# A two-layer recurrent, attention and expert network on one core: the rotation of queries and keys made a lane of its own with one PSUM bank

## The reference, cut to what matters

```python
xn = _layernorm(x)
s = _L0_attn_ref(xn, ...)      # gated recurrence: x@W1, gates, scan over the 512 tokens, @W2
g = _silu(_L0_ffn_ref(xn, ...))  # two layers, below
x = x + s * g
xn = _layernorm(x)
s = _L1_attn_ref(xn, ...)      # 16 heads, all 512 tokens against all 512 tokens
g = _silu(_L1_ffn_ref(...))    # an expert MLP, whose result here is used for one sample
x = x + s * g

def _layer(x, wqkv, qs, ksc, wo, lg, lb, w1, b1, w2, b2):    # run twice
    h = shift_token(x)
    q, k, v = split(h @ wqkv, 3)                 # 8 heads of 64
    q = l2norm(q) * qs;  k = l2norm(k) * ksc
    q, k = rotary_xpos(q, k)                     # rotation by tables of cos and sin
    o = local_attention(q, k, v)                 # windows of 64 tokens and the one before
    x = x + o @ wo
    h = layernorm(shift_token(x)) * lg + lb
    a, g = split(h @ w1 + b1, 2)
    return x + (a * gelu(g)) @ w2 + b2
```

## Time and profile before

| | |
|---|---|
| median of three runs | 3840.28 us |
| the profiled execution: its own time | 3830.7 us |
| the profiled execution: its span | 3828.9 us |
| PE busy | 3102.7 us, 81% |
| DVE busy | 2714.3 us, 71% |
| ACT busy | 2401.6 us, 63% |
| POOL busy | 933.2 us, 24% |
| TensorE clock granted, mean | 0.929 of full |

### The profile page before, as it was taken

The page is one execution under the profiler, slowest core; times in us unless marked ns, Lnnn a source line. Parts: engine busy times, 40 slices in busy tenths (PEclk is TensorE's granted clock), DMA queues, the critical chain, the costliest instruction groups (busy, mean ns, idle before and its releaser), DMA issues.

```text
span 3828.9 us, 55334 instructions
## 1 busy us (share of the span) xinstructions
PE 3102.7 (81%) x19984; PEld 1603.7 (42%) x20144; DVE 2714.3 (71%) x4829; ACT 2401.6 (63%) x5082; POOL 933.2 (24%) x685
## 2 busy tenths in 40 slices
PE   4668787888978787887978888897878789797786
PEld 2444443434444443444444344444444344444241
DVE  3476777868687886868687786868778686868432
ACT  2345666766666675766667676666667676666553
POOL 2021322222122322222132222213232221223100
PEclk7779898999999999999999899999989999999997
DMA  2001000010101001010100101010100101010200
GB/s 68 1 4 46 16 30 32 20 53 16 53 16 50 16 22 47 20 49 20 49 20 26 36 20 53 16 53 16 42 20 20 53 19 50 18 49 13 92 26 11
DMA packets 113451, 122.82 MB, mean 32 GB/s; under 512 B 13427, under 2 KB 86685, under 8 KB 113181
## 3 DMA queue, kind: packets, MB, share of 16 engines
q1 hardware_dynamic: 113180, 119.26, 9.7%
HBM read 64.70 MB, written 54.53 MB: 31 GB/s over the span
## 4 chain that ended last, share of the span: by engine, by line
PE 52%; DVE 26%; ACT 11%; issue 6%; POOL 5%; SPq 1%; DMA 0%; DVEq 0%; POOLq 0%; ACTq 0%
PE pb L573 29%; PE o_bank L573 12%; POOL scratch L1390 4%; DVE nmax L1292 4%; PE s L573 4%; PE pb L668 3%; PE pb L699 2%; DVE stat L1216 2%; ACT ex L1022 2%; DVE scratch L1220 2%; DVE scratch L1196 2%; DVE stat L1186 2%; PE pb L723 2%; DVE side L1158 1%; DVE scratch L1230 1%
## 5 line engine op out<-in xcount | busy, mean ns | idle before, releaser
L1022 ACT ACTIVATE ex<-s,nmax 128x512 f32<-128x512 f32 x1024 | 698.3, 686 | 279.7 <-DVE nmax L1292 257.1
L1292 DVE TENSOR_REDUCE nmax<-s 128x1 f32<-128x512 f32 x1024 | 676.2, 680 | 259.8 <-PE s L573 257.1
L573 PE MATMUL o_bank<-ex,vsc 128*64 128x512 f32 x2048 | 528.2, 638 | 84.6 <-POOL vsc L1424 84.2
L1424 POOL TENSOR_TENSOR vsc<-vrow,rinv 128x256 f32<-128x256 f32 x256 | 157.0, 613 | 1724.2 <-DVE rinv L1300 1724.2
L1385 POOL TENSOR_TENSOR scratch<-scratch 128x1024 f32<-128x1024 f32 x128 | 307.1, 2399 | 564.5 <-DVE scratch L1199 538.5
L573 PE MATMUL s<-qs,ks 96*128 96x512 bf16 x1024 | 345.2, 394 | 82.7 <-ACT ex L1022 82.7
L573 PE MATMUL pb<-wqkv,hsh 128*128 128x512 f32 x768 | 379.1, 622 | 33.8 <-DVE hsh L1179 26.1
L573 PE MATMUL pb<-kT,qT 64*64 64x64 f32 (+1 forms) x6144 | 330.8, 257 | 45.1 <-DVE scratch L1220 12.7
L959 ACT ACTIVATE scratch<-scratch 128x512 f32<-128x512 f32 x256 | 160.7, 628 | 321.1 <-DVE scratch L1220 321.0
L668 PE MATMUL pb<-const,scratch 128*128 128x128 f32 x1024 | 165.3, 308 | 242.2 <-POOL scratch L1390 242.2
L573 PEld LDWEIGHTS pb<-kT,qT 64*64 64x64 f32 x6144 | 282.9, 144 | 98.4 <-issue 98.4
(11 more groups left out here) (190 smaller groups left out, 6108.9 us busy)
## 6 DMA issues: line engine op xcount, KB each, us to landing
parts_store<-side SPq DMA_DIRECT2D x64, 384.0 KB, 2.6
qs<-parts_store SPq DMA_DIRECT2D x128, 192.0 KB, 2.7
ks<-parts_store SPq DMA_DIRECT2D x128, 192.0 KB, 3.2
parts_store<-side SPq DMA_DIRECT2D x64, 256.0 KB, 2.9
parts_store<-side SPq DMA_DIRECT2D x64, 128.0 KB, 2.7
xin<-in_L_attn_x SPq DMA_DIRECT2D x16, 256.0 KB, 3.6
out<-o1T SPq DMA_DIRECT2D x16, 256.0 KB, 4.3
wqkv<-in_L_ffn_wqkv SPq DMA_DIRECT2D x1, 1536.0 KB
```

The lines of the kernel that those rows point to most:

```text
L573: return pe.matmul(o, l, r, start=start, stop=stop, skip_group_check=True)
L1022: A(ex[:, w % 2, j, :], s_bank[(2 * NT + c) % SIMS][:], ACT.Exp, bias=nmax[:, c % 8:c % 8 + 1], accum_out=rsum[:, w % 2, j:j + 1]).then_in ...
L1292: V.tensor_reduce(nmax[:, c % 8:c % 8 + 1], s_bank[(2 * NT + c) % SIMS][:], X, ALU.max, negate=True).then_inc(GV, 1)
L1424: G.tensor_tensor(vsc[:, w % 2].rearrange("p (m a) d -> p m a d", a=2), vrow[:, m:m + 2, 2 * V1 * p:2 * V1 * (p + 1)].rearrange("p m (a d) ...
```

## The change

- The steps from `shift` to `tk` leave `attn0`/`attn1` and become flows `qkv0`/`qkv1`. What stays in `attn` is the score units, `oturn` and `wo`, with unchanged banks A, B, C.
- `q`, `k`, `v`, `tq` and `tk` all use one new bank E. Each waits until the one before has been copied out of it. To make room for E the sims have two banks instead of three.
- Lanes: p is `qkv1`(i-1), `qkv0`(i). r is `attn1`(i-1), `attn0`(i), `post0`(i). s is `pre`(i), `gru`(i-1), `post1`(i-1), `keep0`. g is `glob`(i-2) heads 2 to 15 with its end, `keep1`, then `glob`(i-1) `values` and heads 0 and 1 (FIRST = 2). `expert` moves from iteration 16 to 17, which also holds heads 2 to 15 of the last sample. So an iteration starts with layer 1 of one sample and ends with layer 0 of the next.
- ACT copies q and k out of PSUM at once, and squares both from the copy in one instruction of 128 by 1024. The square is written where the cosine product will be (`l_sq = l_c`), so for t > 0 it waits for the POOL addition of the tile before. `l_qk` has one buffer instead of two, so the copy of q of a tile waits for the sine products of the tile before.
- The score units get scratch of their own (scratch grows from 6144 to 7168 columns); `qT`, `kT`, `va` are still single, so layer 0 of a sample waits piece by piece for the score units of layer 1 of the sample before. `xn0` gets two buffers.
- SP issues the loads of heads 6 to 15 ahead of the stores of the new parts, and the weights of the experts after them.

```diff
-SIMS = 3
+FIRST = 2
-def attn_steps():
+def qkv_steps():
     s = [("shift",)]
...
-    s += [("score", 0), ("rot2", NT - 1), ("tq", NT - 1), ("tk", NT - 1)]
-    units = 2 * NT
+    return s + [("rot2", NT - 1), ("tq", NT - 1), ("tk", NT - 1)]
+
+
+def attn_steps():
+    s, units = [], 2 * NT
     for u in range(units + 4):
-        if 0 < u < units:
-            s += [("score", u)]
         if u < units:
-            s += [("prob", u)]
+            s += [("score", u), ("prob", u)]
...
-    half = s.index(("sim", H1 // 2, 0))
+    half = s.index(("sim", FIRST, 0))
...
-        "a": lane("attn0", 0, STEPS["attn0"]) + lane("post0", 0, STEPS["post0"]) + lane("attn1", 0, STEPS["attn1"]),
-        "s": lane("post1", -1, STEPS["post1"]) + lane("keep0", 0, [("x0",)]) + lane("gru", 0, STEPS["gru"])
-        + lane("pre", 1, STEPS["pre"]),
-        "x": lane("expert", -B, STEPS["expert"][:-1]),
+        "p": lane("qkv1", -1, STEPS["qkv1"]) + lane("qkv0", 0, STEPS["qkv0"]),
+        "r": lane("attn1", -1, STEPS["attn1"]) + lane("attn0", 0, STEPS["attn0"]) + lane("post0", 0, STEPS["post0"]),
+        "s": lane("pre", 0, STEPS["pre"]) + lane("gru", -1, STEPS["gru"]) + lane("post1", -1, STEPS["post1"])
+        + lane("keep0", 0, [("x0",)]),
+        "x": lane("expert", -B - 1, STEPS["expert"][:-1]),
         "g": lane("glob", -2, second) + lane("keep1", -1, [("x1",)]) + lane("glob", -1, values + first),
...
 ORDER = {
-    "pe": ("ga5g2asag2a4gsg5aga2gas3ag3s2a3gsas3gs3a3g3a2g5a2gagsg2ags3g2a2g3agsa2g2as3asg4ag3asa2ga2ga4xg3x4ga2"
...
+    "pe": ("3xgp6xg11xs2gpgs5x2gp2xgsgpgxspgpsgspg4xp2gxrprpxgxprsgxspg7xps2grp3rp2gxp2gxg2xr4xprpgrgx2gxrxrp2xr"
...
+            def qkv_does(l, b, s):                                   # PE
+                f, kind, t = qkv[l], s[0], s[1]
+                if kind in ("q", "k", "v"):
+                    if kind == "v":
+                        need(pe, f, "act", b, ("k", t), "c")
+                    elif kind == "k":
+                        need(pe, f, "act", b, ("q", t), "c")
+                    elif t >= 2:
+                        need(pe, f, "act", b, ("tk", t - 2), "t")
...
+                    mm(bank_e, hsh[:, P * t:P * t + P], wqkv[:, l, INNER * n:INNER * (n + 1)]).then_inc(f.sem["pe"], 1)
...
                 if kind in ("q", "k"):                               # ACT
                     t, k = s[1], int(kind == "k")
-                    src = bank_b if k else bank_a
+                    if t and kind == "q":
+                        need(act, f, "dve", b, ("rot", t - 1), "s1")
                     need(act, f, "pe", b, s, "p")
-                    if t:
-                        need(act, f, "dve", b, ("rot", t - 1), "ss")
-                    A(l_sq[:, INNER * k:INNER * (k + 1)], src, ACT.Square).then_inc(FA, 1)
-                    if t >= 2:
-                        need(act, f, "dve", b, ("rot", t - 2), "s1")
-                    A(l_qk[t % 2][:, INNER * k:INNER * (k + 1)], src, ACT.Copy).then_inc(FA, 1)
+                    A(l_qk[:, INNER * k:INNER * (k + 1)], bank_e, ACT.Copy).then_inc(FA, 1)
+                    if k:
+                        if t:
+                            need(act, f, "pool", b, ("rot", t - 1), "add")
+                        need(act, f, "act", b, s, "c")
+                        A(l_sq, l_qk, ACT.Square).then_inc(FA, 1)
...
-                    if c >= SIMS:
-                        need(pe, glob, "act", b, ("sim", (c - SIMS) // 4, (c - SIMS) % 4), "e")
+                    if c >= 2:
+                        need(pe, glob, "act", b, ("sim", (c - 2) // 4, (c - 2) % 4), "e")
```

246 lines of the change are left out of this document (123 added, 123 removed).

## The result

The changed kernel took 3775.77 us (median of four runs, 3771.37 to 3777.48), the kernel before beside it 3839.36 us: ratio 0.9834, 95% interval 0.9816 to 0.9851. It is faster by 1.7%, where 4.2% were forecast. The profiled execution has a span of 3769.6 us.

The account below looks back on a forecast made before the run. The kernel was taken as bound by the chain attn0, post0, attn1. Parts of 116, 74 and 22 us sum to 212, taken as T = 210; 734 + 14 T gives 3674, forecast 3680 us, range 3570 to 3860.

Parts of the forecast that it names:

- The rotation's waits go nearly whole: PE's waits for the rotation's transposes, 13.5 us an iteration before the change, should vanish almost entirely.
- Part 1, 116 us: From q of layer 1 to post1's start: bound by DVE, 105.7 us of work at a busy share of 0.91.
- Part 2, 74 us: Post1 to its last qk, with the rest of attn0: PE's share makes 70, post1's own chain 74, taken.
- Part 3: Post0 with values and two heads: 22 us as in the kernel before, its order nearly unchanged.
- Some slack of 8 us between the parts: PE can run ahead into post1's stretch; set against 3 us for two score banks and 5 for bank E.
- Squares at nothing: One square from SBUF for two saves 1 us of ACT an iteration, counted as nothing; its wait for POOL taken as 0.
- PE busy 183 us, idle 36: Reading of one iteration of the kernel before: PE works 183.0 us and idles 36, of which 13.5 are the rotation's transposes.
- rival 1: Whole iteration: with the chain broken PE fills up, 201 us (183.0 at 0.91), total 3560; chance 0.14.
- The ends, 734 us: Outside the 14 full iterations: 48.6 + 119 + 192 + 194 + 180 us, against 753 before.
- DVE's dense part 1: Layer 1 to post1: DVE collides with POOL, stretch 125 us, iteration 226, total 3908, slower; chance 0.16.
- bank E as the bound: Rotation's bank: forty hand-overs uncovered by 1 to 1.5 us each, iteration 250 to 270 us, 4240 and more; chance 0.03.
- nothing given in the middle: New chain attn1, post1, post0 replaces the old, post1 filling 100 us: iteration 218 to 220, total 3800 to 3825; chance 0.17.

Follow-up runs that it names:

- e3: Changed kernel with eight DVE instructions of the recurrence's gates and scan on 64 of 512 tokens, 9.7 us of DVE less an iteration: 3757.1 us, ratio 0.9792.
- e5: Changed kernel with three ACT instructions of the recurrence on 64 of 512 tokens, some 3.0 us of ACT less an iteration: 3806.9 us, ratio 0.9926.
- e4: Changed kernel with the recurrence's eight matmuls on 64 of 512 columns, some 6 us of PE less an iteration: 3775.4 us, ratio 0.9843.
- e1: Changed kernel with one of eight matmuls in the 16-head attention's projection, 6.1 us of PE less an iteration: 3714.3 us, ratio 0.9685.
- e8: Changed kernel with another order in post0, y ahead of more of the sims, work unchanged: 3774.7 us, ratio 0.9846.
- e15: Changed kernel with maximum and exp of the eight sims in post0 on 64 of 512 columns: 3716.0 us, ratio 0.9684.
- e17: Changed kernel with bank E as third score bank for two of post0's eight sims, order there nearly as in e8: 3732.1 us, ratio 0.9725.
- e14: Changed kernel with ACT's four copies per tile out of bank E cut to 64 of 512 columns: 3746.3 us, ratio 0.9739.
- e16: Changed kernel with q and k squared straight from PSUM ahead of each copy, into a buffer of their own: 3808.4 us, ratio 0.9909.
- e7: Changed kernel with an own buffer for the squares, so that they no longer wait for POOL's addition: 3765.5 us, ratio 0.9815.
- e6: Kernel before, with q and k copied out of PSUM at once and one instruction squaring both copies: 3949.2 us, ratio 1.0294.

## Why the prediction was wrong, step by step

3680 was forecast, 3776 measured. 14 x 6.25 = 88 us of the 96 lie in the full iterations, 8 in the ends.

- *The rotation's waits go nearly whole*: right, 13.5 us to none.
- *Part 1, 116 us*: right in size, 113.7. Wrong in its cause: it was worked out as DVE's work at a share of 0.91. DVE did 96.7 us of it, not 105.7, and 9.7 us less of its work gave 1.5 us (e3). What bounds the part stays open: DVE does not, ACT's 3 us less gave nothing (e5), and in e4 the clock fell with PE's work, so PE is not ruled out.
- *Part 2, 74 us*: right in size, 73.3. Again another cause: I took post1's chain and scaled PE's 74 us down to 66, since "matmuls overlap". PE was busy for 70.7 there, and e1 shows that PE sets most of it. The factor 183/205 was wrong.
- **Part 3, "as now, 22 us", with "its order nearly unchanged": this is the step that failed.** It is 29.2, and these 7.2 us are more than the 6.25 by which an iteration was missed (parts 1 and 2 were 3 us under, the 2 us taken off the sum did not come). The text ahead of it had named one cause, three sims together with two banks, and I priced all two-bank waits of an iteration at 3 us; the waits for exps rose by 4.4, from 4.9 to 9.3. In post0 3.3 us were lost up to `y`, 1.1 in `y` at a lower clock, and 2.8 behind it: the stretch now holds an `av` and two sims more ahead of layer 1's copy (PE busy for 23.5 us there, against 18.8 in the earlier trace rows) and three maxima on DVE, which I did not count. e8, e15 and e17 show the two banks to be one cause: a third one for two of the eight sims gives back 1.6 us of post0 and 2.5 of an iteration. The maxima ahead of the copy were not tried alone, so how the other 5.6 us of post0 divide is worked out from the timeline and not shown by a run.
- *Some slack of 8 us between the parts* against 3 + 5 us for the banks: the parts sum to 216.2, so no slack is left over. Bank E shows 4.2 us of waits where 5 were taken; with its copies cut to an eighth the iteration lost 1.4 (e14), at a lower clock.
- *The clock*: no term of the sum. Five of the 14 iterations have part 1 at 0.91 and are 3.5 us longer than the others, which is 1.2 of the 6.25 us: the other nine average 215.0.
- *Squares at nothing*: wrong. In the changed kernel copying first is worth 2.9 us an iteration (e16 against e7); in the order of the kernel before the same edit costs 7.6 (e6: 227.7 from one `hsh<-x` to the next, before 220.1). That the wait for POOL costs 0 was right (e7).
- *PE busy 183 us, idle 36*: some 4 of the 36 are the ten matmuls of score units without a record. The rotation's share of PE's idle time was a little larger than read, and rival 1, from 183 at 0.91, should have been some 4 us an iteration slower.
- *The ends, 734 us*: 742. The single terms were far off and cancelled: iteration 0 took 124 (119), iteration 1 208 (192), iteration 16 190 (194), iteration 17 171 (180). In iteration 1 layer 1 took 113 us up to post1's `mlp_in` (173.2 to 286.3), where I had 96 from a stretch of the kernel before (167.5 to 264); post1 took 65 for 74, post0 30 for 22.
- *By the Trainium skill, Perfetto Trace Analysis, section Matmuls, groups should rotate through different banks.* I weighed that rule for bank E, where other lanes' matmuls mostly cover it (4.2 us of waits). It bore on the two score banks in post0, where three sims stand together: rotating two of the eight through a third bank gave 44 us.

Of the rivals, DVE's dense part 1 (slower) and bank E as the bound did not come. PE at its limit is shown for part 2 alone. The measured time lies in the stretch that I had given to "nothing given in the middle" (3768 to 3840 us, chance 0.17), but not by that rival's mechanism, since post1 ran its 73 us beside layer 0 as forecast.

## What to carry to other kernels

When a change takes a buffer from one loop to give it to another, price the loop that lost it at the place where its steps stand closest together, not by an average over all of them. Compare what stands between the same two marks in both orders by count of instructions before calling a stretch "unchanged". Less work on one engine may buy almost nothing, and a moved step is worth measuring alone: several at once cost 45 us, one of them alone, on top of the third bank, gave 30. Before a difference of one or two us an iteration is put down to an edit, list the iterations one by one with their granted clock: of those 30 us, 7 are the step at the same clock and the rest are long iterations that no longer came.
